# A hand-laid order of operations for five engines, laid anew in a Gated-DeltaNet layer

## What is computed

```
x = x + layernorm(attn(layernorm(x)))        # x: 4 x 1024 x 256, float32
x = x + layernorm(ffn(layernorm(x)))         # ffn: silu(x Wg) * (x Wu), then Wd; weights = lut[index]

attn:  q, k (16 heads), v (32 heads), 128 wide = silu(conv4(x Wqkv));  z = x Wz
       q, k = l2norm(q), l2norm(k);  beta = sigmoid(x Wb);  g = cumsum of -exp(A_log)*softplus(x Wa + dt)
       A  = -(beta k k^T * decay), strictly lower;   T = (I - A)^-1
       per chunk c, in order:  v_new = T (beta v) - T(beta k exp g) S
                               out   = (q exp g) S + (q k^T * decay) v_new
                               S     = S exp(g_last) + (k exp(g_last - g))^T v_new
       out = out * rsqrt(mean(out^2) + eps) * norm_w * silu(z);   y = out Wout
```

## Time and profile before

| | us |
|---|---|
| median of 3 runs | 5220.78 (5212.98 to 5223.16) |
| the profiled execution's own time | 5225.77 |
| its span, first to last instruction | 5223.6 |
| PE / PEld busy | 4793.1 / 3484.8 (92% / 67%) |
| DVE busy | 3982.4 (76%) |
| ACT / POOL busy | 2669.1 / 2687.3 (51% / 51%) |
| 16 DMA queues busy, mean | 18% in the main part |

### The profile page before, as it was taken

One profiled execution on the slowest core, in us unless ns is written; L12 is line 12 of the kernel. 1 busy time (PEld: TensorE's weight loads), 2 busy tenths in 40 slices (PEclk: granted clock), 3 DMA queues, 4 the chain that ended last, 5 costly groups with the idle time before them and its releaser, 6 DMA issues. The chain is left out here.

```text
span 5223.6 us, 98451 instructions
## 1 busy us (share of the span) xinstructions
PE 4793.1 (92%) x33236; PEld 3484.8 (67%) x33236; DVE 3982.4 (76%) x8539; ACT 2669.1 (51%) x5425; POOL 2687.3 (51%) x8582
## 2 busy tenths in 40 slices
PE   4799999999999999999999999999999999998698
PEld 2477777676767677777777777777777777776344
DVE  4588887887778778878888888888887788875464
ACT  2355555555555555555555555555555555554111
POOL 0455665555555555556655565655566555654000
PEclk8799999999999999999999999999999999999899
DMA  3121111221111111111211111121121121110200
GB/s 121 35 42 38 35 42 38 45 49 30 41 46 39 32 41 40 42 39 39 44 47 44 35 38 39 41 50 42 32 49 43 38 44 36 38 38 22 90 17 17
DMA packets 579248, 219.42 MB, mean 42 GB/s; under 512 B 455212, under 2 KB 541612, under 8 KB 577080
## 3 DMA queue, kind: packets, MB, share of 16 engines
q1 hardware_dynamic: 578744, 213.13, 17.7%
HBM read 161.02 MB, written 52.00 MB: 41 GB/s over the span
## 5 line engine op out<-in xcount | busy, mean ns | idle before, releaser
L428 PE MATMUL pp<-xnT,W 128*128 128x512 f32 x2048 | 1006.2, 621 | 109.2 <-DVE CV L718 77.7
L718 DVE SCALAR_TENSOR_TENSOR CV<-pp,CW,CV 128x1023 f32<-128x1023 f32 (+2 forms) x768 | 980.3, 1276 | 58.0 <-ACT CV L1002 46.2
L1222 POOL TENSOR_TENSOR TM<-UL,XL 128x126 f32<-128x126 f32 (+22 forms) x1984 | 703.2, 354 | 279.1 <-issue 120.3
L1225 POOL TENSOR_TENSOR UL<-UL,TM 128x126 f32<-128x126 f32 (+22 forms) x1984 | 736.8, 371 | 155.4
L428 PEld LDWEIGHTS pp<-xnT,W 128*128 128x128 f32 x2048 | 377.7, 197 | 432.4 <-issue 389.2
L852 DVE TENSOR_TENSOR CO<-qa,QE 128x256 f32<-128x256 f32 x512 | 215.5, 421 | 450.8 <-PE qa L582 448.8
L1002 ACT ACTIVATE CV<-pp,CW 128x1024 f32<-128x1024 f32 x256 | 284.4, 1111 | 483.1 <-PE pp L428 483.1
L616 PE MATMUL emit<-Wo,NTr 128*128 128x256 f32 x2048 | 529.1, 404 | 0.8 <-ACT NTr L1131 0.8
L1259 POOL TENSOR_TENSOR tv<-SC,EQ 128x4 f32<-128x4 f32 x256 | 51.7, 202 | 917.6 <-DVE SC L860 917.6
L1086 ACT ACTIVATE QE<-qa,TAB 128x128 f32<-128x128 f32 x1024 | 319.5, 365 | 398.4 <-PE qa L553 398.2
L595 PE MATMUL emit<-Wz,xnT 128*128 128x256 f32 x2048 | 495.7, 385 | 3.4 <-DVE OACC L892 3.2
(11 more groups left out here) (197 smaller groups left out, 9936.7 us busy)
## 6 DMA issues: line engine op xcount, KB each, us to landing
W<-wqkv SPq DMA_DIRECT2D x256, 128.0 KB, 3.1
XL<-xb SPq DMA_DIRECT2D x128, 256.0 KB, 4.0
xb<-X SPq DMA_DIRECT2D x512, 32.0 KB, 1.6
UL<-c_u SPq DMA_DIRECT2D x64, 256.0 KB, 2.7
ub<-UL SPq DMA_DIRECT2D x128, 128.0 KB, 3.0
N<-ub SPq DMA_DIRECT2D x256, 64.0 KB, 2.2
Wz<-wz SPq DMA_DIRECT2D x64, 256.0 KB, 2.6
Wo<-wo SPq DMA_DIRECT2D x64, 256.0 KB, 3.2
```

The lines of the kernel that those rows point to most:

```text
L428: ins = t.matmul(bk.pp[:, 512 * h:512 * h + 512], m.W[:, c, k, :], m.xnT[:, w // KH % 2, c, 512 * h:512 * h + 512], start=c == 0, stop=c == 1)
L718: v.scalar_tensor_tensor(m.CV[:, t, d:S], bk.pp[:, 0:S - d], m.CW[:, w % KH, t, 3 - d:4 - d], m.CV[:, t, d:S], ALU.mult, ALU.add).then_inc ...
L1222: p.tensor_tensor(m.TM[:, 0:a, 0:b], m.UL[:, 0:a, k:k + 1].to_broadcast([128, a, b]), m.XL[:, k, k + 1:32].unsqueeze(1).to_broadcast([128, ...
L1225: p.tensor_tensor(m.UL[:, 0:a, k + 1:32], m.UL[:, 0:a, k + 1:32], m.TM[:, 0:a, 0:b], ALU.subtract).then_inc(s["sub"], 1)
```

## The change

No instruction is added, removed or resized by hand. The calls of each engine's list are put in another order, `TURN` follows, and some calls move to the neighbouring iteration, with u shifted by one: `at`, `ks`, `qs`, `vn` of the last chunks (TensorE), `state`, `core`, `r_`, `lm` (VectorE), `qe(u, 7)` (ScalarE), `vsc(u, 1)`, `nk`, `la`, `ixf` (GpSimd), `ui`, `ldz`, `ldw(., 1)`, `decoded` (SyncE). The order was laid by a planner that was told longer durations for everything outside TensorE.

VectorE, from chunk 4:

```diff
         ulr(u, 1)
         r_(u, 4)
+        red(u, 1)
         oacc(u, 0)
-        red(u, 1)
+        seed(u, 1)
         state(u, 4)
-        seed(u, 1)
         core(u, 4)
-        r_(u, 5)
         mk(u + 2, 0)
         kred(u + 2)
+        r_(u, 5)
+        x(u + 2, 0)
+        att(u + 2, 0)
+        lm(u + 1, 2)
         nrm(u, 1)
-        x(u + 2, 0)
-        vt(u + 1)
         state(u, 5)
```

ScalarE, around the table loads, and GpSimd at the end of its list and over its start:

```diff
+        dec(u + 2, 0)
+        qe(u, 5)
         sz(u, 1)
-        qe(u, 5)
-        dec(u + 2, 0)
...
         qe(u, 6)
+        dec(u + 2, 1)
         cv0(u + 2, 2)
+        y1l(u + 1, 0)
         vs(u, 6)
-        dec(u + 2, 1)
         vne(u, 6)
-        y1l(u + 1, 0)
         sz(u, 2)
...
         on(u - 1, 2)
+        vsc(u, 1)
+        nk(u + 1)
+        la(u + 1, 0)
+        la(u + 1, 1)
         tv(u - 1, 3)
...
         on(u, 1)
+        la(u + 1, 2)
         vsc(u + 1, 0)
-        vsc(u + 1, 1)
-        ixf(u + 1)
+        la(u + 1, 3)
         tv(u, 2)
-        nk(u + 2)
+        ixf(u + 2)
```

More of the change, by code:

```diff
@@ L68, in tile_count @@
     return 4 * w + t
-TURN = (("dec", 1, 3), ("kq", 1, 3), ("tpv", 1, 0), ("tpv", 1, 1), ("tpv", 1, 2), ("tpv", 1, 3), ("tpq", 2, 0),
-        ("tpq", 2, 1), ("tpk", 2, 0), ("tpk", 2, 1), ("dec", 2, 0), ("kq", 2, 0), ("dec", 2, 1), ("kq", 2, 1),
-        ("dec", 2, 2), ("kq", 2, 2))
+TURN = (("kq", 1, 2), ("dec", 1, 3), ("kq", 1, 3), ("tpv", 1, 0), ("tpv", 1, 1), ("tpv", 1, 2), ("tpv", 1, 3),
+        ("tpq", 2, 0), ("tpq", 2, 1), ("tpk", 2, 0), ("tpk", 2, 1), ("dec", 2, 0), ("kq", 2, 0), ("dec", 2, 1),
+        ("kq", 2, 1), ("dec", 2, 2))
 FIRST = -3
@@ L394, in main_sp @@
     for u in range(-4, NU + 2):
+        index(u + 1)
         xo(u + 1, 0)
-        ldz(u)
         xo(u + 1, 1)
-        ui(u + 1)
         xl(u + 1)
-        index(u + 1)
-        ldw(u + 2, 1)
+        ldg(u + 2)
+        ldo(u)
+        ldz(u + 1)
         ldt(u + 1)
         ldw(u + 2, 2)
-        ldo(u)
         ldw(u + 2, 3)
         ldw(u + 3, 0)
[L407 to L410, removed]
         uo(u + 1)
         nl(u + 1)
+        ui(u + 2)
+        ldw(u + 3, 1)
+        ldx(u + 4)
+        decoded(u + 1)
+        sto(u - 2)
     sp.wait_ge(s["dwd"], 16 * KH)
@@ L621, in main_pe @@
         m2(u, 0)
+        at(u - 1, 6)
+        ks(u - 1, 7)
+        kq(u + 1, 2)
+        qs(u - 1, 7)
+        m3(u, 0)
         ctp(u - 1, 2)
-        sup(u - 1, 7)
-        at(u - 1, 7)
+        vn(u - 1, 7)
         decp(u + 1, 3)
         op(u - 1, 2)
-        qs(u, 0)
         kq(u + 1, 3)
-        m3(u, 0)
+        at(u - 1, 7)
+        pj(u + 1, 3, 0)
+        sup(u - 1, 7)
+        m4(u, 0)
         z(u - 1, 3)
         ks(u, 0)
-        m4(u, 0)
-        pj(u + 1, 3, 0)
+        qs(u, 0)
         pj(u + 1, 3, 1)
+        tpv(u + 1, 0, 0)
+        vn(u, 0)
+        m1(u, 1)
         ctp(u - 1, 3)
[L636 to L639, removed]
         sup(u, 0)
         tpv(u + 1, 0, 1)
+        at(u, 0)
         op(u - 1, 3)
+        qs(u, 1)
         ks(u, 1)
-        qs(u, 1)
         pj(u + 2, 0, 0)
@@ L1133, in main_act @@
     for u in range(-4, NU + 2):
[L1134 to L1137, removed]
         u12l(u, 0)
         u12r(u, 0)
+        dec(u + 1, 2)
+        qe(u - 1, 7)
+        nt(u - 1, 2)
+        vs(u - 1, 7)
+        y2(u, 0)
+        vne(u - 1, 7)
+        dec(u + 1, 3)
         sq(u - 1, 3)
-        dec(u + 1, 3)
-        y2(u, 0)
         sz(u - 1, 3)
@@ L1145, in main_act @@
         cv0(u + 1, 3)
+        vev(u + 1, 0, 0)
         vs(u, 0)
         vne(u, 0)
-        vev(u + 1, 0, 0)
+        y1l(u, 1)
         nt(u - 1, 3)
-        y1l(u, 1)
         qe(u, 1)
@@ L1153, in main_act @@
         vne(u, 1)
+        cv0(u + 2, 0)
+        sq(u, 0)
+        u12l(u, 1)
+        qe(u, 2)
         vev(u + 1, 0, 1)
[L1155 to L1158, removed]
         u12r(u, 1)
+        vs(u, 2)
+        vne(u, 2)
+        sz(u, 0)
         vev(u + 1, 1, 0)
         y2(u, 1)
-        vs(u, 2)
-        sz(u, 0)
-        vne(u, 2)
+        qe(u, 3)
         qt(u + 2)
         cv0(u + 2, 1)
-        qe(u, 3)
-        vev(u + 1, 1, 1)
         vs(u, 3)
         vne(u, 3)
+        vev(u + 1, 1, 1)
         qsq(u + 2, 0)
         nt(u, 0)
+        sq(u, 1)
         qe(u, 4)
@@ L1175, in main_act @@
         kt(u + 2)
-        sq(u, 1)
+        kev(u + 2, 0)
         vs(u, 4)
-        kev(u + 2, 0)
         vne(u, 4)
@@ L1299, in main_pool @@
         sub(u + 1, 5)
+        ng(u + 1)
         sub(u + 1, 6)
@@ L1310, in main_pool @@
         sub(u + 1, 15)
+        tv(u, 0)
         sub(u + 1, 16)
```

118 lines of the change are left out of this document (52 added, 66 removed).

## The result

The changed kernel takes 4868.09 us (4866.2 to 4872.72), the kernel before, run beside it, 5221.97 (5212.98 to 5228.8): ratio 0.9325, 95% interval 0.9308 to 0.9341, 354 us less. The prediction was 5045 with a range down to 4920: right in sign, half of the size, and outside its range.

What follows compares the result with a forecast made beforehand. TensorE's queue was taken to set the pace. Per unit, 72.64 - 2.09 - 1.08 - 1.45 + 0.5 + 0.5 + 0.4 + 0.4 = 69.8 us; 64 x 2.8 = 180 us less gave 5045 us, range 4920 to 5190.

Steps and rivals of the forecast that it cites:

- The two waits: TensorE's waits at the transpose of quarter 1 (2.09 us a unit) and the second projection (1.08) were to be mended.
- The norm held by la and vsc: At quarter 1 the norm loses some 2.1 us to GpSimd, leaving the transpose a 0.5 us wait a unit.
- slower, by the port lock: Rival: vsc calls hold output norms in full, delaying ctp(u,1) and decp(u+1,3), 7.9 us a unit, 5400 us; chance 0.14.
- sup(u,4): On TensorE in chunk 4, less work between vn and sup leaves a pause: loss 0.5 us a unit.
- Table loads and decp(u+1,3): At an iteration's start, extra ScalarE table loads delay x and att before decp: loss 0.4 us a unit.
- Clock: TensorE's lowered clock costs 1.45 us a unit and goes with the waits, with 0.4 left.
- The rest, taken as 0: All other changed places, such as state to ks, r_ to vn and SyncE loads, were counted as no change.
- that is the floor for any order of the same work: A unit without TensorE's idle time and clock loss takes 67.5 us, claimed as the least possible.
- The wait only moves: Rival: VectorE is late at another place for each one mended, unit 72.6 us, 5220 us; chance 0.06.
- clean sweep: Rival: all new waits hide and the clock stays full, 4890 to 4895 us (range 4885 to 4990); chance 0.18.

Runs made afterwards that it cites:

- b_vsc_late: Kernel before with one added wait: both vsc calls start only after the norm of quarter 1, no longer beside kred; 5045.27 us, ratio 0.9646.
- b_taps_first: Kernel before with cv0(u+2,0) earlier on ScalarE, the second tap earlier and seed(u,0) later on VectorE; 5210.52 us, ratio 0.9974.
- a_four_loads: New kernel with ScalarE's sz(u,1), qe(u,5), dec(u+2,0) in old order and dec(u+2,1) later, for four table loads a unit; 5161.59 us, ratio 0.988.
- b_both: Kernel before with the edits of b_vsc_late and b_taps_first together; 5044.74 us, ratio 0.9646.
- b_four: b_both plus r_(u,3) ahead of nrm(u,0) and state(u,5) ahead of vt(u+1) on VectorE; 5128.88 us, ratio 0.9816.
- b_nine: b_both plus VectorE swaps, TensorE and ScalarE chunks 2 to 4 in new order, vt(u+1) behind r_(u,6), m1(u+1,0) behind vn(u,6); 5169.07 us.
- b_five: b_both plus r_(u,3) ahead of nrm(u,0) on VectorE and TensorE's chunk 3 as in the new kernel; 5064.17 us, ratio 0.9668.
- a_vsc_pair: New kernel with both vsc calls right behind on(u,1), ahead of la(u+1,2) and the norm of quarter 1; 4956.64 us, ratio 0.9478.
- a_lm_early: New kernel with lm(u+1,2) ahead of x and att of quarter 0 on VectorE; 4863.08 us, ratio 0.9308.
- a_chunk3_back: New kernel with TensorE's order from sup(u,3) to qs(u,4) as before; 4961.54 us, ratio 0.9493.

## Why the prediction was right or wrong

A ledger of the unit, before against after. Idle is what the stretch has over TensorE's busy time; the clock is what is lost to it, 104.2 us before and 1.7 after; the rest of the busy time is what is left.

| us a unit | before | after | gain | predicted gain |
|---|---|---|---|---|
| TensorE idle | 3.71 | 0.40 | 3.31 | 3.17 - 1.4 (new waits) |
| clock | 1.66 | 0.03 | 1.63 | 1.05 |
| rest of its busy time | 67.27 | 66.53 | 0.74 | 0 |
| unit | 72.64 | 66.96 | 5.68 | 2.8 |

*The two waits* (2.09 and 1.08): right. b_vsc_late and b_taps_first each take one away, though in the old order only the first brings time. The cause of the first, kred held by vsc, is shown by b_vsc_late. The times were met as well: from sup(u,4) at 2537.20, kred starts at +2.29 (forecast +2.35), the norm ends at +8.61 (+8.65 without lock), TensorE comes at +10.22 (+10.5).

*The norm held by la and vsc* (+0.5): less than 0.1. This is the first step that failed: "one of its four instructions waits out la, the next the vsc". In 57 of 62 units none of the four does; la stands beside all four (1.51 us), and the vsc comes after them. In the other five it goes as predicted, the norm loses 2.1 us and TensorE waits 0.5 to 0.8. So the size of the lock and of the wait were right, and how often they come was wrong. The start times do not tell the two kinds of unit apart (la 0.23 us behind the norm in both), and in a_four_loads, with the same 0.23 us, all 62 go as predicted. That this term came to almost nothing is luck as far as the runs show. The same holds for the rival "slower, by the port lock" (0.14): a norm held in full with 1.9 us of wait and the slow clock behind it is what a_four_loads does, at 5162 us, three moved calls away from the new kernel.

*sup(u,4)* (+0.5): there, 1.46 us from vn to sup. But TensorE's wait for VS is 1.9 us in the whole stretch; the pause is within "busy", and what else went from there outweighs it.

*Table loads and decp(u+1,3)* (+0.4): the second step that failed. The loads came (188 and 186), the wait didn't: decp waits 0.6 us in all. The step counted only what the loads might delay, and not what the earlier exp makes room for: 1.3 us ahead of the transpose (a_four_loads).

*Clock* (1.45, 0.4 left): 1.66, nothing left. The 1.45 came from a clock that the view rounds to 0.98. The 0.4 was for short waits that bring a slow stretch, and those waits hardly came.

*The rest, taken as 0*: the third step that failed, and the largest single miss. The busy time itself fell by 0.74 us a unit at the same work, although the pause at sup(u,4) came into it, and of the 0.54 us of idle time outside the two waits 0.2 went. That the 0.74 are short waits that the busy records held is inferred, not measured one by one. One trace of them is to be read in the weight loads: ks for St, before and after,

```profile
PEld kv L543 <- DVE St L841: 51.4, 195, 0.7
```

```profile
PEld kv L543 <- DVE St L841: 0.5, 2, 0.2
```

With it falls "that is the floor for any order of the same work": 67.5 was reckoned from busy time that still held such pauses (and from the rounded clock, 0.2), and the new order went 0.5 under it. The Trainium skill (Perfetto Trace Analysis, Identifying the Most-Contended Engine) calls the busy share of matmuls no good measure of how close TensorE is to its limit, because pipelined instructions look smaller than they are. The ledger agrees that it is no good measure, but for another reason: the busy time of the kernel before was too long, by 0.74 us a unit.

*The rivals.* "The wait only moves" was given 0.06 and taken for a remote case. For nearly every partial version of this change it is what happens (b_taps_first, b_both, b_four to b_nine). For the whole it doesn't: the new order has room at all these places at once. Where the 177 us between b_vsc_late and the new kernel lie can be told only in part. With the other lists new, putting back TensorE's chunk 3 costs 93; b_five, with that stretch in the old order, is no faster than b_both. Where the cause of these 177 us lies, and which smallest set of edits gives them, stays open.

*The distribution.* Three of the four losses in the sum (the norm, decp, the clock that was left) came out at next to nothing and the fourth was outweighed. The clean sweep had been argued for in its own words, "every new wait above is within 0.5 us of being hidden", and got 0.18. Its time rested on the wrong floor, and the range was cut off at 4920, inside that case.

## What to carry to other kernels

When a hand-laid order is replaced as a whole, price the old order's losses as idle time plus clock plus the short waits within busy records, and give the case in which the new order has them all back a fair chance; here it had nearly all. Single swaps in the old order are no measure of it: here most only handed the wait on to the next place. Look first for a short instruction that takes several times its shortest, and for the long one of another engine beside it: here one added wait on one semaphore was worth 180 of 354 us. Before calling an added instruction, such as a table load, a cost, ask what its new place lets start earlier.

## What the runs showed of the hardware

Either engine can be the one that stands at the port between VectorE and GpSimd. Where GpSimd's instruction had a clear start, VectorE's stood: the norm took 3.26 us instead of 1.13 beside two vsc (a_vsc_pair), 2.20 beside one that had run for 0.63 us (a_lm_early). Where the norm's first instruction started 0.23 us ahead of la, and la 0.03 us ahead of the norm's second, both outcomes are on record. In the new kernel la stood beside all four instructions of the norm in 57 of 62 units (1.51 us instead of 0.75). In four of the other five, and in all 62 units of a_four_loads, la ran at once and the norm's second instruction stood (0.87 us instead of 0.35); in the fifth la stood for 0.24 us and then the norm's third. The kernel before has 47 norms with la 0.23 us behind them, and in all of them the second instruction stands. One of them, with la at 1023.03 and 0.75 us long:

```profile
1022.53 0.35 DVE L903 TENSOR_SCALAR wv<-ix,lc 128x268 f32<-128x268 f32 x1
1022.80 1.66 DVE L878 SCALAR_TENSOR_TENSOR CO<-CO,ty,SZ 128x128 f32<-128x128 f32 x4
```

What decides between the two was not found; the distances lie between 0.22 and 0.24 us with either outcome. By the Trainium skill (SBUF — State Buffer, Who interferes with whom) the one that issues first has the port for its whole instruction and the other stands. The trace agrees where one had a clear start and in the units where the norm's second instruction stood. That la stands through four VectorE instructions, three of which started after it, does not follow from the rule.

How much of the lower clock a short wait brings differs widely. b_five has two of about 0.9 us a unit and loses 7 us to the clock in its profiled execution; a_vsc_pair with one of 0.8 us loses 7 as well. b_nine with one of 0.95 us and three of 0.4 on average loses 107, as much as the kernel before (104) with its one of 2 us and one of 1.1. And a kernel at full clock can still lose 93 us to three waits of 0.3 to 0.6 us (a_chunk3_back). What tells b_five and b_nine apart was not settled.
